# Layer 0 attention on TensorE: scores and values as 32-row and 32-column pieces, values one slot later, the minimum with zero as a relu on ScalarE

## What is computed

```
q = (layernorm(x) @ Wq + bq)   # 16 heads of 16
k = (context @ Wk + bk)        # 77 keys
v = (context @ Wv + bv)
attn = clip(q k^T * 0.25, -10000, 10000)
attn = softmax(attn)           # over the 77 keys, per head
x = x + tanh(g) * ((attn v) @ Wo + bo)
```

## Time and profile before

| | |
|---|---|
| median of 3 runs | 1470.08 us (1467.53 to 1470.77) |
| the profiled execution's own time | 1470.64 us |
| its span, first to last instruction | 1468.9 us |
| mean granted TensorE clock | 0.921 |
| PE busy in the span | 1260.1 us (86%), 8531 instructions |
| DVE busy | 1052.2 us (72%) |
| ACT busy | 801.2 us (55%) |
| POOL busy | 582.4 us (40%) |
| layer 0 attention, about 12 to 333 us of the span | 321 us |

### The profile page before, as it was taken

How to read it: one execution, slowest core, us unless ns; L and a number is a source line. 1 busy time by engine, 2 the same in 40 slices (tenths; PEclk the granted TensorE clock), 3 DMA queues, 4 the chain that set the end, 5 groups by cost and what they waited for, 6 DMA issues and landing times. The chain is left out here.

```text
span 1468.9 us, 27990 instructions
## 1 busy us (share of the span) xinstructions
PE 1260.1 (86%) x8531; PEld 943.4 (64%) x8578; DVE 1052.2 (72%) x2148; ACT 801.2 (55%) x2378; POOL 582.4 (40%) x599
## 2 busy tenths in 40 slices
PE   3989998986349999999999979957898888949898
PEld 2878787873137777777777744945666656634466
DVE  3988888866655555555555531648999989948898
ACT  2555454542135564555555522636677666727898
POOL 3666666653152222222232100036877767620000
PEclk9999999997659999999999985979999999978999
DMA  3122222217011111111111141020111111100033
GB/s 107 63 84 87 85 86 86 79 47 233 1 51 41 54 43 51 49 43 54 46 46 54 36 137 42 1 61 29 58 59 52 58 52 50 37 19 1 1 109 121
DMA packets 74070, 88.60 MB, mean 60 GB/s; under 512 B 9677, under 2 KB 64323, under 8 KB 73859
## 3 DMA queue, kind: packets, MB, share of 16 engines
q1 hardware_dynamic: 66529, 68.66, 14.7%
q0 software_dynamic: 6816, 18.62, 4.9%
q10 hardware_dynamic: 642, 0.33, 0.1%
HBM read 60.58 MB, written 27.00 MB: 60 GB/s over the span
## 5 line engine op out<-in xcount | busy, mean ns | idle before, releaser
L1078 ACT ACTIVATE exp_h<-exp_ps_h,exp_b_now 128x256 f32<-128x256 f32 x312 | 128.8, 463 | 180.1 <-PE exp_ps_h L1018 176.1
L1018 PE MATMUL exp_ps_h<-exp_xhi,exp_w_now 128*128 128x256 bf16 x1248 | 215.2, 276 | 5.8 <-DVE exp_xlo L1104 5.8
L1612 ACT ACTIVATE a_z<-a_ps_sc,a_nmx 128x77 f32<-128x77 f32 x512 | 159.2, 367 | 98.8 <-DVE a_nmx L1729 98.8
L1122 DVE TENSOR_TENSOR exp_hlo<-exp_h,exp_hhi 128x512 bf16<-128x512 f32 x156 | 107.9, 691 | 95.2 <-ACT exp_hhi L1082 95.2
L1018 PE MATMUL exp_ps_h<-exp_xlo,exp_w_now 128*128 128x256 bf16 x624 | 172.2, 276 | 0.0
L1030 PE MATMUL exp_ps_y<-moe_w2s,exp_hhi 128*128 x585 | 139.2, 379 | 2.0
L1018 PEld LDWEIGHTS exp_ps_h<-exp_xhi,exp_w_now 128*128 128x128 bf16 x1248 | 123.6, 99 | 22.0 <-issue 4.0
L1612 ACT ACTIVATION_READ_ACCUMULATOR a_z<-a_ps_sc,a_nmx 128x1 f32 x512 | 127.7, 249 | 0.0
L1579 PE MATMUL a_ps_o<-a_v_now,a_phi 128*128 128x256 bf16 (+1 forms) x640 | 119.2, 292 | 7.8 <-DVE a_plo L1718 7.6
L986 POOL COPY exp_at_now<-all_token_of 128x2 int32 (+1 forms) x39 | 17.0, 435 | 254.8 <-PE exp_ps_x L1005 252.4
L992 POOL DMA_INDIRECT exp_xg<-xn,exp_at_now x78 | 92.8, 1189 | 41.3 <-POOL exp_at_now L986 29.4
(11 more groups left out here) (250 smaller groups left out, 3083.5 us busy)
## 6 DMA issues: line engine op xcount, KB each, us to landing
a_stage<-in_L_ffn_W_dram SPq DMA_DIRECT2D x64, 256.0 KB, 3.0
y_slots<-exp_y SPq DMA_DIRECT2D x78, 128.0 KB, 1.8
a_x<-in_x_dram SPq DMA_DIRECT2D x32, 128.0 KB, 2.1
x<-a_xo SPq DMA_DIRECT2D x32, 128.0 KB, 1.7
route_x<-x SPq DMA_DIRECT2D x8, 512.0 KB, 7.7
xn<-route_x SPq DMA_DIRECT2D x8, 512.0 KB, 3.0
a_x<-x SPq DMA_DIRECT2D x32, 128.0 KB, 2.2
x<-a_xob SPq DMA_DIRECT2D x32, 128.0 KB, 1.7
```

What stands on the lines that cost most here:

```text
L1018: mm = pe.matmul(ps_h[:, i, f % 2 * SLOT_T:(f % 2 + 1) * SLOT_T], w1_now[:, v, k, hl, f * P:(f + 1) * P], xx[:, k, :], start=(q == 0), sto ...
L1078: ins = act.activation(h[:, f, :], ps_h[:, i, f % 2 * SLOT_T:(f % 2 + 1) * SLOT_T], ACT.Gelu_apprx_tanh, bias=b1_now[:, v, f:f + 1])
L1122: dve.tensor_tensor(hlo[:, v, 2 * i:2 * i + 2, :].rearrange("p f t -> p (f t)"), h[:, 2 * i:2 * i + 2, :].rearrange("p f t -> p (f t)"), h ...
L1612: ins = act.activation(z[:, u, h * KEYS:(h + 1) * KEYS], ps_sc[:, j, (h - SB[j][0]) * KEYS:(h - SB[j][0] + 1) * KEYS], ACT.Exp, bias=nmx[: ...
```

## The change

The head groups are cut once more. LANES = 4 lanes of 32 features (2 heads) per group: the scores of a lane use the 32 rows 32j to 32j+31 of qT and of kblk, which now has 2 x 77 columns per group, and write to the lane's own PSUM bank: 8 matmuls of 32 rows and 154 columns in place of 4 of 128 rows. z then holds the heads in the order of lanes. The values of a pair of heads are 32 columns; 17 (piece, pair) blocks of 32 weight columns in place of 11 of 128, each written to the lane's 32 partitions of PSUM, taken in turns over the lanes. kblk is written in 2 instructions instead of 8.

The value projection makes 17 blocks of 32 columns, by 34 matmuls, in slot t = 2; wv is loaded by six DMAs that reorder its columns.

The maximum and the subtraction are one instruction each, over the four banks. The minimum on VectorE goes; ScalarE takes relu(-z), then the exponential with the opposite scale. The residual stands ahead of the sums. The values belong to tile T-3 (pT has two buffers), SKEW is 4; the output projection (T-4) opens TensorE's slot; the last two transposes of P and their copies move behind the transposes of x; the copy of attnT closes ScalarE's slot. ps_p has two banks, ps_sc four.

Constants and blocks:

```diff
-    blocks = blocks_of(hpg)
+    LANES = P // 32
+    PAIR = 2 * KEYS
+    BANK = ng * PAIR
+    blocks = [(c, q) for c in range(RCH) for q in range(ng * LANES) if c * P < (q + 1) * PAIR and (c + 1) * P > q * PAIR]
...
-    RING, SKEW = 8, 3
+    vgroups = [range(0, 16), range(16, len(blocks))]
+    RING, SKEW = 8, 4
```

TensorE, value projection:

```diff
-                    for i, (c, g) in enumerate(group):
+                    for i in group:
+                        c, q = blocks[i]
...
-                            mm = pe.matmul(ps_p[:, j, i * P:(i + 1) * P], ctx_now[0:n, k, at0:at0 + P],
-                                           wv[0:n, k, g * P:(g + 1) * P], start=(k == 0), stop=(k == 1))
+                            mm = pe.matmul(ps_p[:, j, (i - group[0]) * 32:(i - group[0] + 1) * 32], ctx_now[0:n, k, at0:at0 + P],
+                                           wv[0:n, k, q * 32:(q + 1) * 32], start=(k == 0), stop=(k == 1))
```

TensorE, the slot:

```diff
+                if has(T - 4):
+                    pe.wait_ge(s["attn_done"], T - 3)
+                    for g in range(ng):
+                        mm = pe.matmul(ps_o, attnT[:, g, :], wo[:, g, :], start=(g == 0), stop=(g == ng - 1))
+                    mm.then_inc(s["o_done"], 1)
...
                     pe.wait_ge(s["qT_done"], T + 1)
-                    for j, (a, _) in enumerate(SB):
-                        wait(pe, s["z_done"], NSB * (T - 1) + j + 1)
...
-                        mm.then_inc(s["scores_done"], 1)
+                    wait(pe, s["z_done"], T)
+                    for g in range(ng):
+                        for j in range(LANES):
+                            lane = slice(32 * j, 32 * j + 32)
+                            mm = pe.matmul(ps_sc[:, j, g * PAIR:(g + 1) * PAIR], qT[lane, g, :], kblk[lane, g, :],
+                                           start=True, stop=True)
+                    mm.then_inc(s["scores_done"], 1)
                 if has(T + 1):
                     turn_x(T + 1)
                 if has(T - 2):
...
+                    pe.wait_ge(s["pT_done"], 3 * (T - 2) + 1)
+                    turn_p(T - 2, u, 2)
+                if has(T - 3):
...
+                    wait(pe, s["xo_done"], T - 3)
+                    for i in turns:
+                        c, q = blocks[i]
+                        j, g = q // ng, q % ng
...
+                        mm = pe.matmul(ps_v[32 * j:32 * j + 32, g * P:(g + 1) * P], vblk[0:n, i, :], pT[0:n, 1 - u, c, :],
+                                       start=(c == mine[0]), stop=(c == mine[-1]))
                     mm.then_inc(s["pv_done"], 1)
-                if has(T) and t == 1:
+                if has(T) and t == 2:
```

ScalarE, the slot:

```diff
-                if has(T - 3):
-                    act.wait_ge(s["pv_done"], T - 2)
-                    wait(act, s["o_done"], T - 3)
-                    act.activation(attnT[:, :, :].rearrange("p g t -> p (g t)"), ps_v, ACT.Copy).then_inc(s["attn_done"], 1)
                 if has(T - 1):
                     v = (t - 1) % 2
+                    act.wait_ge(s["z_done"], T)
+                    act.activation(z[:, v, :], z[:, v, :], ACT.Relu, scale=-1.0).then_inc(s["zc_done"], 1)
                     act.wait_ge(s["zc_done"], T)
-                    act.activation(z[:, v, :], z[:, v, :], ACT.Exp, scale=scale).then_inc(s["exp_done"], 1)
+                    act.activation(z[:, v, :], z[:, v, :], ACT.Exp, scale=-scale).then_inc(s["exp_done"], 1)
...
+                if has(T - 3):
+                    act.wait_ge(s["pv_done"], T - 2)
+                    wait(act, s["o_done"], T - 3)
+                    act.activation(attnT[:, :, :].rearrange("p g t -> p (g t)"), ps_v, ACT.Copy).then_inc(s["attn_done"], 1)
```

VectorE:

```diff
-                for h in range(hpg):
+                for h in range(2):
                     ins = dve.tensor_scalar(kblk[:, :, h * KEYS:(h + 1) * KEYS],
...
-                if has(T - 1):
-                    sums(T - 1, (t - 1) % 2)
...
+                if has(T - 1):
+                    sums(T - 1, (t - 1) % 2)
                 if has(T):
-                    for j, (h0, h1) in enumerate(SB):
-                        dve.wait_ge(s["scores_done"], T * NSB + j + 1)
...
+                    dve.wait_ge(s["scores_done"], T + 1)
+                    dve.tensor_reduce(mx[:, :].rearrange("p (i x) -> p i x", i=LANES), scores, AX,
+                                      ALU.max).then_inc(s["max_done"], 1)
...
-                    dve.wait_ge(s["z_done"], NSB * (T + 1))
-                    dve.tensor_scalar(z[:, u, :], z[:, u, :], 0.0, None, ALU.min).then_inc(s["zc_done"], 1)
```

More of the change, by code:

```diff
@@ L160, in attention @@
     dh = P // hpg
-    blocks = blocks_of(hpg)
+    LANES = P // 32
+    PAIR = 2 * KEYS
+    BANK = ng * PAIR
+    blocks = [(c, q) for c in range(RCH) for q in range(ng * LANES) if c * P < (q + 1) * PAIR and (c + 1) * P > q * PAIR]
+    lanes = [[i for q in range(ng * j, ng * j + ng) for i, (c, qq) in enumerate(blocks) if qq == q] for j in range(LANES)]
+    turns = [i for row in itertools.zip_longest(*lanes) for i in row if i is not None]
     scale = float(dh) ** -0.5
-    NSB = len(SB)
     ctx_rows = (P, DC - P + 1)
-    pieces = pieces_of(hpg)
-    vgroups = [blocks[i:i + 4] for i in range(0, len(blocks), 4)]
+    vgroups = [range(0, 16), range(16, len(blocks))]
     NVG = len(vgroups)
-    RING, SKEW = 8, 3
+    RING, SKEW = 8, 4
     with ExitStack() as ctx:
@@ L203, in attention @@
         ps_v, ps_o = ps_vo[:, 0:D], ps_vo[:, D:2 * D]
+        scores = ps_sc[:, :, 0:BANK].rearrange("p i (x k) -> p i x k", k=KEYS)
         keys_in, weights_in, gbo_done = m.sem("keys_in"), m.sem("weights_in"), m.sem("gbo_done")
@@ L292, in _ @@
             power(1, 1)
[L293 to L302, removed]
+            pool.affine_select(out=vmask_all[:, :, :], in_=vmask_all[:, :, :], compare_op=ALU.is_ge, fill=0.0, base=0,
+                               pattern=[[P, RCH], [-KEYS, HEADS]], channel_multiplier=1).then_inc(s["mask_step"], 1)
+            pool.wait_ge(s["mask_step"], 5)
+            pool.affine_select(out=vmask_all[:, :, :], in_=vmask_all[:, :, :], compare_op=ALU.is_ge, fill=0.0, base=KEYS - 1,
+                               pattern=[[-P, RCH], [KEYS, HEADS]], channel_multiplier=-1).then_inc(s["mask_step"], 1)
+            pool.wait_ge(s["mask_step"], 6)
+            for c in range(RCH):
+                mine = [i for i, (cc, _) in enumerate(blocks) if cc == c]
+                q0 = blocks[mine[0]][1]
+                pool.tensor_copy(vmask[:, mine[0]:mine[-1] + 1, :].rearrange("p i h -> p (i h)"),
+                                 vmask_all[:, c, 2 * q0:2 * (q0 + len(mine))]).then_inc(s["mask_step"], 1)
             pool.wait_ge(weights_in, 16 * N_WEIGHTS)
@@ L344, in turn_x, with turn_p @@
                 mm.then_inc(s["turned_x"], 1)
+            def turn_p(T, u, j):
+                for c in range(4 * j, min(RCH, 4 * j + 4)):
+                    n = min(P, ROWS - c * P)
+                    mm = pe.transpose(ps_p[0:n, j % 2, c % 4 * P:(c % 4 + 1) * P], z[:, u, c * P:c * P + n], C.ident[:, :])
+                mm.then_inc(s["turned_p"], 1)
             def keys(T, b):
@@ L384, in slot @@
                     pe.wait_ge(s["norm_done"], T - 1)
-                    if t == 2:
+                    if t == 3:
                         pe.wait_ge(s["v_done"], NVG * (b + 1))
[L387 to L393, removed]
-                if has(T - 3):
[L395 to L398, removed]
+                    wait(pe, s["pT_done"], 3 * (T - 2))
+                    for j in range(2):
+                        turn_p(T - 2, u, j)
                 if has(T):
                     pe.wait_ge(s["qT_done"], T + 1)
-                    for j, (a, _) in enumerate(SB):
-                        wait(pe, s["z_done"], NSB * (T - 1) + j + 1)
[L403 to L407, removed]
-                        mm.then_inc(s["scores_done"], 1)
+                    wait(pe, s["z_done"], T)
[5 more added lines that the diff above has]
+                    mm.then_inc(s["scores_done"], 1)
                 if has(T + 1):
```

117 lines of the change are left out of this document (58 added, 59 removed).

## The result

The changed kernel took 1480.9 us (median of 5 runs, 1477.0 to 1483.9) against 1469.2 for the kernel before (5 runs): a ratio of 1.0084, 95% interval 1.0058 to 1.0109. It is slower. The forecast was 1461; the time lies inside the range, but on the side on which I had put 4 chances in 10. The profiled execution took 1479.02 us, with a span of 1477.2 (before 1468.9).

A forecast was written before the change was run, and what follows sets the result against it. Bound: the exponential, then nearly all VectorE does, in an 8.24 us slot. Regular slots -7.1, batch ends and value projections -4.7, end +2.6 give -9.2: 1461 us. Forecast's own range 1454 to 1470; with rivals 1441 to 1500.

The forecast's parts named there:

- The clamp stays 0.43: VectorE, regular slot: the clamp between maximum and subtraction was to keep its 0.43 us.
- the ring of 7.59: VectorE's cycle in a regular slot: relu, exponential, sum and reciprocal, maxima, clamp, subtraction, together 7.59 us.
- The merged maxima and the moved residual: VectorE, regular slot: single maximum and subtraction to save 0.25 us together, the residual ahead of the sum 0.40.
- Relu for minimum: ScalarE's relu at 1.23 us, handoff 1.27, replacing VectorE's minimum of 1.23: no gain, perhaps 0.4 us cost.
- Pieces s = 1.15, p = 1.93: TensorE: streaming time of the cut scores (s, 1.15 us) and values (p, 1.93 us), assuming partial overlap of lanes.
- Rival 1: Full overlap of the four lanes on TensorE, s = 0.6, p = 1.0, VectorE bounding the slot: 1442 us, chance 0.2.
- The ring of 8.01 through the values: Regular slot: the prediction's 8.01 us ran through relu, qT, scores, maximum, clamp and subtraction; its cycle through the values was 7.89.
- Changes of the array's shape, 0.3 each: TensorE, cycle through the values: two changes of tiling shape, taken at 0.3 us each.
- Batch ends, regular: Slots ending a batch: two kblk instructions (0.7 us) beside the relu, 0.3 us excess kept for each of three ends.
- Value projection, 7.3 us at 0.107 each, slot 14.5: TensorE: 68 projection records at the weight load's pitch of 0.107 us, 7.3 us in all, their slot 14.5 long.
- Rival 4: The granted clock falls to 1.2 GHz in the value projection, 68 records taking 15 us: 1498 us, chance 0.12.
- Start 0 and end +2.6: Attention's start taken as 0, between minus 2 and plus 3 us; its end 2.6 us longer, a tile passing one slot more.

The follow-up runs named there:

- e5: The changed kernel with the maxima written to free PSUM columns, where the clamp reads them: 1456.1 us, ratio 0.989 to the kernel before.
- e4: The changed kernel with 68 projection records streaming up to 128 columns in place of 32, some value blocks wrong: 1458.9 us, ratio 0.992 to the kernel before.
- e7: The changed kernel with maxima in PSUM and 40 projection records, all streaming 128 columns: 1422.1 us, ratio 0.968 to the kernel before.
- e11: The changed kernel with maxima in PSUM and 40 projection records of narrow columns (32 to 96): 1428.6 us, ratio 0.972 to the kernel before.
- e8: The changed kernel with scores and values issued lane by lane in place of turns: 1484.5 us in one execution.

## Why the prediction was wrong, step by step

- **"The clamp stays 0.43", and the ring of 7.59 built on it: the step that failed.** I read the clamp's duration as work. Rows show 0.43 for 16 elements where the residual's 256 take 0.48, and the line's minimum of 0.17 was in the trace; I read neither. The ring through GpSimd (8.22) was never drawn, because the chain showed no semaphore between GpSimd and the clamp. It costs 31 x 0.85 = 26 us against the slot that e5 shows (7.37).
- **The merged maxima and the moved residual** (0.65 on the ring): right in size, as e5's slot of 7.37 shows against 7.33 worked out, but hidden behind the normalisation.
- **Relu for minimum, "gives nothing on the ring":** right for the duration (1.23). But the minimum's 1.23 was partly the same wait, and its 0.80 at the least was the sign of it.
- **Pieces s = 1.15, p = 1.93:** wrong; 0.81 and 1.29 whole, with the tail of about 0.3 in both. Rival 1 was right on the mechanism, and on VectorE's wait: it idled 0.99 for the exponential at 240.52. It was wrong on the time (1442), for the clamp's sake and for the projection's. The ring of 8.01 through the values never bound.
- **Changes of the array's shape, 0.3 each:** too high, as far as the trace shows: the most is 0.19, the idle time of the weight path before the values.
- **Batch ends, regular:** right (8.12 at 99.65 to 107.77).
- **Value projection, 7.3 us at 0.107 each, slot 14.5:** near the mark at the full clock (e4: 7.86, slots of 12.3 to 14.6), wrong as the clock fell. Rival 4 had 15 us at a chance of 0.12; two projections took 14.7 and two 10.7. Excess of the four slots: 77.8 in all, less 4 x 8.175 (the mean of the other slots), is 45.1 us against 24.4 with the ends.
- **Start 0 and end +2.6:** the first relu starts 1.2 us sooner than the first minimum did (31.8 in the earlier trace rows), and the stretch from the last z to the routing is 0.6 longer. The last values start 12.0 us after the last z (13.1 forecast, 9.9 before) and take 1.4 us less.

The sum, on the profiled executions: regular slots 31 x (8.175 - 8.01) = +5.1, projections +20.7, start -1.2, end -2.0 against their terms. That is 22.6, and 23.0 if the slots of before are counted from minimum to minimum (284.1 us), as start and end are, in place of exponential to exponential (284.5); 17.6 was missing (1479.0 against 1461.4). The other 5.4 us came back behind the attention, in stages that the change doesn't touch. They take 1130.5 us after and 1136.1 before, counted from the routing's first instruction; over the variants of the change 1130.5 to 1133.8, over those of the kernel before 1134.4 to 1136.2. I haven't found out why.

In short: the shorter VectorE ring was hidden by a wait that no semaphore names, and the projection's slots cost 45 us of excess where the kernel before had 29 in all. Part of the nearness to the forecast was luck. The slot of 8.01 came within 0.2 of the measured 8.175 because two errors cancelled: the pieces were taken too slow, so that the ring through them stood where no ring was, and the wait of the clamp, which was in no term and no rival, filled its place. With the pieces right and the wait left out the forecast would have been a slot of 7.59.

## What to carry to other kernels

Compare each small instruction's duration with its own minimum and with its size. Where 16 elements take 0.4 or 1.0 us, look at what GpSimd ends at that moment, and draw that ring too. Put a small VectorE step on the critical path beside a GpSimd instruction so that it reads PSUM, or let GpSimd start behind it. When matmuls are cut up, count records and look at the granted clock of the stretch: 68 narrow ones took up to twice the time of 68 wide ones (14.7 against 7.9), and 40 of either kind, with the clamp in PSUM, hid half behind the slot.

## What the runs showed of the hardware that was not expected

- A 128x16 clamp within SBUF took 0.17 us alone and 1.03 beside a GpSimd instruction that had 1.0 us still to go; reading PSUM it took 0.17 all 32 times. The wait shows as duration, not as idle time.
- Float32 matmuls on 32-row pieces in four lanes: 16 records of 154 columns in 0.81 us, where the whole form took 2.34 for 8 records (two each of 462 and 154 columns, four of 308), 1232 columns in both forms. That is full overlap, as near as the trace tells: the estimate for it was 0.51 of streaming and 0.3 for the tail. Values in 32-column pieces took 1.29 in turns over the lanes and 2.68 lane by lane.
- The granted clock was 0.50 over 122 to 137 us of the change, in which TensorE had no idle time, and stayed at the full level over the same projection with the same number of wide records (e4).
- Every trace starts at half pace: before, the key projection's 8 records took 1.96 us at 17.57 and 1.01 at 91.44. The trace has no record of the clock until that ends, at 28.5 us in the kernel before, 38.6 in the change, 39.4 in e7, 50.7 in e4, 57.8 in e11 and 64.6 in e8, and the clock's column says 1.00 for the time without a record. So in e11's first projection the records stood 0.218 apart under a column of 1.00, and the first projections of e4, e8 and e11 can't be compared with those of other runs by that column; the 0.93 of e4 for 12 to 340 us holds such time too. Why the slow start lasts longer in one run than in another is not shown.
